# Second layer of a two-layer transformer: batch 0's residual inside batch 1's operand stage, batch 1's residual and the last normalisation as one stage

## The reference

```python
x = x + _layernorm(_L0_attn_ref(_layernorm(x), ...))
x = x + _layernorm(_L0_ffn_ref(_layernorm(x), ...))
x = x + _layernorm(_L1_attn_ref(_layernorm(x), ...))
x = x + _layernorm(_L1_ffn_ref(_layernorm(x), ...))
```

## Time and profile before

| | us |
|---|---|
| three runs, median (lowest, highest) | 3185.22 (3184.61, 3186.84) |
| profiled execution, its time | 3187.83 |
| profiled execution, its span | 3186.0 |

### The profile page before, as it was taken

How to read it: one execution, slowest core, us unless ns; L and a number is a source line. 1 busy time by engine, 2 the same in 40 slices (tenths; PEclk the granted TensorE clock), 3 DMA queues, 4 the chain that set the end, 5 groups by cost and what they waited for, 6 DMA issues and landing times. The chain is left out here.

```text
span 3186.0 us, 42804 instructions
## 1 busy us (share of the span) xinstructions
PE 2862.2 (90%) x14636; PEld 2289.0 (72%) x14636; DVE 1879.3 (59%) x3604; ACT 1231.7 (39%) x2366; POOL 990.2 (31%) x780
## 2 busy tenths in 40 slices
PE   7969999789999999458999999857999999499998
PEld 5846666568787878347788888656888888378886
DVE  5647787574453545445566666655666666644446
ACT  2226666562122212232444444322444444243334
POOL 1217777655453636305000000032000000122223
PEclk9979999889999999679999999979999999789999
DMA  4774444142121201671001000030000000300012
GB/s 165 239 212 142 121 129 125 56 142 83 42 64 41 64 24 34 212 291 74 18 23 35 23 23 35 29 140 28 24 23 35 23 23 30 126 21 20 10 37 80
DMA packets 138035, 244.06 MB, mean 77 GB/s; under 512 B 14417, under 2 KB 78929, under 8 KB 137393
## 3 DMA queue, kind: packets, MB, share of 16 engines
q1 hardware_dynamic: 137904, 242.40, 23.4%
HBM read 162.92 MB, written 79.17 MB: 76 GB/s over the span
## 5 line engine op out<-in xcount | busy, mean ns | idle before, releaser
L1094 POOL TENSOR_TENSOR l0a_probs_hl<-l0a_probs,l0a_probs_hl 128x896 fp32r<-128x896 f32 (+1 forms) x128 | 285.0, 2244 | 108.1 <-ACT l0a_probs L1022 108.1
L1352 ACT ACTIVATE l1a_probs<-l1a_scores,l1a_row 128x128 f32<-128x128 f32 (+7 forms) x256 | 189.6, 742 | 317.9 <-DVE l1a_row L1389 317.8
L1326 PE MATMUL l1a_obank<-l1a_pT_hl,l1k_v_hl 128*128 128x512 f32 (+3 forms) x1152 | 300.4, 370 | 7.2 <-DVE l1a_pT_hl L1399 7.1
L1442 POOL TENSOR_TENSOR l1a_q_stage<-l1k_qpe,l1a_ones 128x512 fp32r<-128x512 f32 x32 | 33.3, 1041 | 875.3 <-PE l1a_work L1334 818.4
L1399 DVE TENSOR_TENSOR l1a_pT_hl<-l1a_work,l1a_pT_hl 128x512 fp32r<-128x512 f32 (+3 forms) x384 | 213.2, 555 | 154.6 <-ACT l1a_pT_hl L1359 154.4
L1306 PE MATMUL l1a_scores<-l1k_kT_hl,l1a_qa_hl 128*128 128x512 f32 (+3 forms) x1152 | 291.6, 361 | 1.5 <-ACT l1a_probs L1352 1.5
L1359 ACT CAST l1a_pT_hl<-l1a_work 128x512 fp32r<-128x512 f32 (+3 forms) x384 | 183.7, 478 | 106.3 <-PE l1a_work L1317 105.2
L1334 PE MATMUL l1a_work<-l1a_wov,l1a_oT_hl 128*128 128x512 f32 x768 | 214.3, 401 | 5.0 <-DVE l1a_oT_hl L1418 3.0
L1389 DVE TENSOR_REDUCE l1a_row<-l1a_scores 128x1 f32<-128x128 f32 (+7 forms) x256 | 190.0, 751 | 44.5 <-PE l1a_scores L1309 44.4
L1413 DVE SCALAR_TENSOR_TENSOR l_acc<-l1a_work,l1a_row,l_acc 128x512 f32<-128x512 f32 x256 | 189.4, 750 | 34.4 <-PE l1a_work L1334 24.5
L1713 PE MATMUL f0f_ybank<-f0f_wT,f0f_h_hl 128*128 128x512 f32 x768 | 196.7, 406 | 12.7 <-POOL f0f_h_hl L1879 12.6
(11 more groups left out here) (255 smaller groups left out, 6200.0 us busy)
## 6 DMA issues: line engine op xcount, KB each, us to landing
v_dram<-l0f_v_rows SPq DMA_DIRECT2D x24, 768.0 KB, 4.0
qk_dram<-l0f_stage SPq DMA_DIRECT2D x128, 128.0 KB, 2.5
l1a_wov<-wov_dram SPq DMA_DIRECT2D x32, 512.0 KB, 3.4
l0a_v_stage<-v_dram SPq DMA_DIRECT2D x32, 384.0 KB, 4.3
l1a_wabs<-wabs_dram SPq DMA_DIRECT2D x32, 384.0 KB, 3.8
l0a_q_stack<-qk_dram SPq DMA_DIRECT2D x32, 256.0 KB, 3.6
l0a_k_stack<-qk_dram SPq DMA_DIRECT2D x32, 256.0 KB, 3.8
f0f_chunk<-in_L_ffn_w_gate_up SPq DMA_DIRECT2D x32, 256.0 KB, 2.7
```

What stands on the lines that cost most here:

```text
L1094: nc.gpsimd.tensor_tensor(probs_hl[:, r, 1, 0:wide], probs[:, r, 0:wide], f32(probs_hl[:, r, 0, 0:wide]), ALU.subtract).then_inc(low_done, 1)
L1326: last = pe.matmul(obank[:, c:SPAN], src["v_hl"][:, a, n, :], pT_hl[:, ring(n, s), b, c:SPAN], start=(n == 0 and i == 0), stop=(n == QT * ...
L1352: nc.scalar.activation(probs[s][:, first:first + wide, :].rearrange("p k c -> p (k c)"), scores[:, n % S_AHEAD, 0:wide * P], ACT.Exp, bias ...
```

## The change

- Batch 0's `residual` stage after its attention is dropped. `latent_operands` for batch 1 gets `rows`: per tile the statistics, a root on ScalarE, the inverse and a shift (minus mean times inverse) on VectorE, the row scaled by ScalarE in place in `acc`, the sum with `x2` on GpSimd in place, a store to `x3`. The two accumulators become one, `l1_acc`.
- Batch 1's `residual` stage and the `norm_transposed` before the feed-forward become `residual_norm_transposed`. Tiles of batch 0 come from `x3` (kind A), tiles of batch 1 from `acc` after their residual (kind B), in the order of `join_order`. Rows of both kinds are scaled by ScalarE.
- In `feed_forward` the last rows are scaled and summed in place in `acc`; the buffer `z` and its waits for stores go.

```diff
+def join_order():
+
+    order = [("A", k) for k in range(QT)]
+    for k in range(TB - QT):
+        order += [("A", QT + k), ("B", k)]
+    return order + [("B", k) for k in range(TB - QT, TB)]
...
+def residual_norm_transposed(nc, m, ident, done_rows, acc, src, dst, xT_hl, loads):
...
+            def inverse(which, n):
+                r = n % RING
+                dve.wait_ge(std_done[which], n + 1)
+                nc.vector.reciprocal(rstd[:, which, r:r + 1], std[:, which, r:r + 1]).then_inc(rstd_done[which], 1)
+                dve.wait_ge(rstd_done[which], n + 1)
+                nc.vector.scalar_tensor_tensor(out=shift[:, which, r:r + 1], in0=mv[:, which, r, 0:1], scalar=-1.0,
+                                               in1=rstd[:, which, r:r + 1], op0=ALU.mult, op1=ALU.mult
+                                               ).then_inc(shift_done[which], 1)
+
+            for i in range(N + LATER + 4):
+                j = i - LATER
+                if i < TB:
+                    statistics(0, i, acc[:, i, :])
+                if 0 <= j < N:
+                    kind, k = order[j]
+                    if kind == "A":
+                        dve.wait_ge(x0_loaded[k // QT], 16)
+                    else:
+                        dve.wait_ge(sum_done, k + 1)
+                    statistics(1, j, source(j))
+                if 0 <= i - 1 < TB:
+                    inverse(0, i - 1)
+                if 0 <= j - 1 < N:
+                    inverse(1, j - 1)
+                if i < TB:
+                    aggregate(0, i)
+                if 0 <= j < N:
+                    aggregate(1, j)
+                if 0 <= j - 4 < N:
+                    j = j - 4
+                    dve.wait_ge(high_done, j + 1)
+                    nc.vector.tensor_tensor(xT_hl[:, 1, :, tokens(j)],
+                                            bank[:, j % RING, :].rearrange("p (k t) -> p k t", k=KT),
+                                            f32(xT_hl[:, 0, :, tokens(j)]), ALU.subtract).then_inc(low_done, 1)
+            dve.wait_ge(low_done, N)
...
+            def scaled(which, n, to, rows):
+                r = n % RING
+                act.wait_ge(shift_done[which], n + 1)
+                return nc.scalar.activation(to, rows, ACT.Identity, bias=shift[:, which, r:r + 1],
+                                            scale=rstd[:, which, r:r + 1])
+
+            for i in range(N + LATER + 4):
+                if 0 <= i - 1 < TB:
+                    root(0, i - 1)
+                if 0 <= i - LATER - 1 < N:
+                    root(1, i - LATER - 1)
+                if 0 <= i - 2 < TB:
+                    k = i - 2
+                    scaled(0, k, acc[:, k, :], acc[:, k, :]).then_inc(z_done, 1)
+                if 0 <= i - LATER - 2 < N:
+                    j = i - LATER - 2
+                    wait(act, turned, j - 1)
+                    scaled(1, j, xn[:, j % 2, :], source(j)).then_inc(normed, 1)
+                if 0 <= i - LATER - 4 < N:
+                    j = i - LATER - 4
+                    act.wait_ge(turned, j + 1)
+                    nc.scalar.copy(xT_hl[:, 0, :, tokens(j)], bank[:, j % RING, :].rearrange("p (k t) -> p k t", k=KT)
+                                   ).then_inc(high_done, 1)
+
...
+                pool.wait_ge(z_done, k + 1)
+                pool.wait_ge(x1_loaded[k // QT], 16)
+                nc.gpsimd.tensor_tensor(acc[:, k, :], acc[:, k, :], x1[:, k, :], ALU.add).then_inc(sum_done, 1)
...
-                    wait(act, row_stored[b], 16 * half)
-                    nc.scalar.activation(z[:, b, :], acc[:, half * QT + b, :], ACT.Identity,
+                    nc.scalar.activation(acc[:, half * QT + b, :], acc[:, half * QT + b, :], ACT.Identity,
...
+def latent_operands(nc, m, ident, xT_hl, waT, wpT, norm_w, rope, out, stores=(), rows=None):
...
+            def load_row(t):
+                wait(sp, r_sum_done, t - 1)
+                sp.dma_start(x[:, t % 2, :], row_src[t * P:(t + 1) * P, :]).then_inc(r_loaded[t % 2], 16)
+
             for dst, tile in stores:
                 sp.dma_start(dst, tile).then_inc(stored, 16)
+            if rows is not None:
+                load_row(0)
+                load_row(1)
+                for t in range(TB):
+                    sp.wait_ge(r_sum_done, t + 1)
+                    sp.dma_start(row_dst[t * P:(t + 1) * P, :], acc[:, t, :]).then_inc(r_stored, 16)
+                    if t + 2 < TB:
+                        load_row(t + 2)
+                sp.wait_ge(r_stored, 16 * TB)
...
-            act.wait_ge(eps_set, 1)
-            for i in range(TB + 1):
+            act.wait_ge(eps_set, 1 if rows is None else 2)
+            for i in range(TB + 2):
+                if rows is not None and 1 <= i <= TB:
+                    t = i - 1
+                    act.wait_ge(r_mv_done, t + 1)
+                    nc.scalar.activation(r_std[:, t % 2:t % 2 + 1], r_mv[:, t % 3, 1:2], ACT.Sqrt, bias=eps_ln[:, 0:1]
+                                         ).then_inc(r_std_done, 1)
+                if rows is not None and i >= 2:
+                    t = i - 2
+                    act.wait_ge(r_shift_done, t + 1)
+                    nc.scalar.activation(acc[:, t, :], acc[:, t, :], ACT.Identity, bias=r_shift[:, t % 2:t % 2 + 1],
+                                         scale=r_inv[:, t % 2:t % 2 + 1]).then_inc(r_z_done, 1)
                 if i < TB:
                     t = i
                     act.wait_ge(d_full, t + 1)
...
+                if rows is not None and i < TB:
+                    t = i
+                    nc.vector.bn_stats(r_stats[:, t % 2, :], acc[:, t, :]).then_inc(r_stats_done, 1)
+                if rows is not None and 1 <= i <= TB:
+                    t = i - 1
+                    dve.wait_ge(r_std_done, t + 1)
+                    wait(dve, r_z_done, t - 1)
+                    nc.vector.reciprocal(r_inv[:, t % 2:t % 2 + 1], r_std[:, t % 2:t % 2 + 1]).then_inc(r_inv_done, 1)
+                    dve.wait_ge(r_inv_done, t + 1)
+                    nc.vector.scalar_tensor_tensor(out=r_shift[:, t % 2:t % 2 + 1], in0=r_mv[:, t % 3, 0:1], scalar=-1.0,
+                                                   in1=r_inv[:, t % 2:t % 2 + 1], op0=ALU.mult, op1=ALU.mult
+                                                   ).then_inc(r_shift_done, 1)
+                if rows is not None and i < TB:
+                    t = i
+                    dve.wait_ge(r_stats_done, t + 1)
+                    nc.vector.bn_aggr(r_mv[:, t % 3, :], r_stats[:, t % 2, :]).then_inc(r_mv_done, 1)
...
+                        pool.wait_ge(r_z_done, t + 1)
+                        pool.wait_ge(r_loaded[t % 2], 16 * (t // 2 + 1))
+                        nc.gpsimd.tensor_tensor(acc[:, t, :], acc[:, t, :], x[:, t % 2, :], ALU.add
+                                                ).then_inc(r_sum_done, 1)
...
                     kept.close()
                     with phase(f"l1a{b}") as m:
-                        attention_layer1(nc, m, ident, ident_bf, mask, ops, acc)
-                with phase(f"l1r{b}") as m:
-                    residual(nc, m, TB, x2[b * S:(b + 1) * S], x3[b * S:(b + 1) * S], lambda t: acc[:, t, :])
...
                 with phase("f1n") as m:
-                    norm_transposed(nc, m, ident, x3, NT, xT,
-                                    group_loads(raw1, 0, 0, *ffn1) + group_loads(raw1, 1, 1, *ffn1))
+                    residual_norm_transposed(nc, m, ident, x3[0:S], l1_acc, x2[S:2 * S], x3[S:2 * S], xT,
+                                             group_loads(raw1, 0, 0, *ffn1) + group_loads(raw1, 1, 1, *ffn1))
+                acc = x.sb("acc", [P, NT, D])
```

More of the change, by code:

```diff
@@ L1848, in run @@
                     dve.wait_ge(x_loaded[half % 2], 16 * (half // 2 + 1))
-                    nc.vector.tensor_tensor(z[:, b, :], z[:, b, :], x[:, half % 2, b, :], ALU.add).then_inc(sum_last, 1)
+                    row = acc[:, half * QT + b, :]
+                    nc.vector.tensor_tensor(row, row, x[:, half % 2, b, :], ALU.add).then_inc(sum_last, 1)
         each_group(dve, run, chunks is not None, rows is not None)
@@ L1898, in run @@
                     pool.wait_ge(x_loaded[half % 2], 16 * (half // 2 + 1))
-                    nc.gpsimd.tensor_tensor(z[:, b, :], z[:, b, :], x[:, half % 2, b, :], ALU.add).then_inc(sum_done, 1)
+                    row = acc[:, half * QT + b, :]
+                    nc.gpsimd.tensor_tensor(row, row, x[:, half % 2, b, :], ALU.add).then_inc(sum_done, 1)
         each_group(pool, run, chunks is not None, rows is not None)
@@ L2172, in latent_operands @@
     stored = m.sem("stored")
+    if rows is not None:
+        row_src, row_dst, acc = rows
+        x = m.sb("x", [P, 2, D])
+        r_stats, r_mv = m.sb("r_stats", [P, 2, 6]), m.sb("r_mv", [P, 3, 2])
+        r_std, r_inv, r_shift = (m.sb(n, [P, 2]) for n in ("r_std", "r_inv", "r_shift"))
+        eps_ln = m.sb("eps_ln", [P, 1])
+        r_loaded = [m.sem(f"r_loaded{i}") for i in range(2)]
```

(9 more changed lines are left out.)

83 lines of the change are left out of this document (74 added, 9 removed).

## The result

The changed kernel takes **3170.14 us** (median of five runs, 3168.19 to 3173.05), the kernel before 3185.22 (3184.29 to 3194.30) beside it. The ratio of the runs is 0.9948, 95% interval 0.9934 to 0.9963: faster by 0.5%. The prediction said 3173, range 3164 to 3181. The profiled execution has a span of 3168.4 us, 17.6 under that of before; its own time is the median.

The account below looks back on a forecast made before the run. TensorE, busy nine tenths of the span, was taken as the bound, with gains only where it stands still. -19.4 + 17.1 - 9.7 - 0.3 = -12.3 us gave a median of 3173 us, range 3164 to 3181.

Parts of the forecast that it names:

- Part 1: Between batch 0's attention and batch 1's norm stage: the residual stage goes, 19.4 us gained (bounds 18.7 and 20.1).
- Part 2: Batch 1's operand stage, which takes in batch 0's residual: 17.1 us paid (bounds 9.8 and 25).
- The loop: Operand stage: copy, VectorE's round, aggregate, square root, scaled row, next copy take 10.1 us instead of 7.93.
- Five steps: Operand stage: five of seven steps from copy to copy contain the rotary part, 5 x 2.15 = 10.8 us.
- the last two tiles: End of the operand stage: its last two rounds cost about 0.4 us more.
- rival C: Operand stage: TensorE falls to its lower clock, six rounds 35 us longer than forecast, 3208 us, slower; chance 0.04.
- The choice between a held and a free shift: Operand stage: shift taken as held until GpSimd's sum ends, 2.5 us after the crossing; free it ends after 1.0.
- A: Rival, operand stage: the shift isn't held by GpSimd's sum, residual costs 9.8 us, whole 3166 us; chance 0.15.
- Part 3: Joined stage of batch 1's residual and the norm: 47.0 us instead of 56.75, 9.7 gained (bounds 39 and 54).
- the eight rounds with both chains: Joined stage: 8 rounds at 3.1 us from the first layer's output stage, less early subtractions, 22.1 us.
- The tail: End of the joined stage, after the last aggregate: root, inverse, row, transposes, copy, subtraction and handovers, 3.7 us.
- Part 4: Feed-forward's rows in place: one wait for a store goes from the last group, 0.3 us gained.

Follow-up runs that it names:

- root_later: Against the changed kernel, ScalarE issues the residual's root and scaled row behind the casts of the operand stage's round: 3159.76 us, ratio to the kernel before 0.9914.
- shift_one_input: Against the changed kernel, the one-column shift is a tensor_scalar with one SBUF tensor in operand and joined stages: 3156.79 us, ratio to the kernel before 0.9904.

## Why the prediction was right, step by step

- **Part 1**, 19.4 us gained: 20.71 - 1.40 = 19.3. The handover with clearing took 1.4 where 1.3 was taken. The norm stage (b) kept its length, so the table load costs nothing.
- **Part 2**, 17.1 us paid: 18.2. The loop was 9.96 us for 10.1. Five steps gave 5 x 2.03 = 10.1 (10.8 less the 0.7 of VectorE's wait), the two before them 4.52 + 6.00 - 3.11 - 4.49 = 2.9 (3.3), the end 3.6 - 0.3 = 3.3 (3.4). The mis-sized term is the last two tiles, taken at 0.4: from the last copy to the end of the last rotary sum it is 25.7 us for 23.5, so 2.2. There TensorE was at its lower clock for a part of the products: the last two groups took 5.71 and 5.97 us for 4.36 each before (last section). The first copy came 0.3 us sooner after its product's start. It was rival C in a small form: not a loop at the lower clock, but two groups of products; in the rounds from 2123 to 2153 the granted clock was 1.00. What the prediction held against C, that waits of 2 to 2.6 us had left the clock at 1.00, didn't carry over: the group of 5.97 us stands behind the same wait of 2.60 us.
- **The choice between a held and a free shift**, on which A stood, was right: median 1.80 us. That root_later took back 12.9 us of part 2 by the order, and shift_one_input 7.2 by the shift, shows both links of the loop. A's own price of 9.8 us doesn't follow from its loop of 8.8: five steps of 1.3 us less take 6.5 off 17.1 and leave 10.6. With free shifts, in shift_one_input, stage (c) paid 87.44 - 76.39 = 11.05.
- **Part 3**, 47.0 us: 45.7. Handover 1.45 (1.3), 5.8 to the first rows of x (5.5). From there to the end of the last aggregate at 2777.7 it is 32.9 (35.7): 20.7 for the eight rounds with both chains (22.1) and 12.2 for the eight with one (13.6). Of the first eight, three went by before GpSimd's first add (2750.31) in 1.0, 1.9 and 1.9 us; the five after it took 2.5 to 4.3 us, 3.2 in the mean, with the seven held shifts (0.65 to 1.24 us each) among them. The 3.1 us a round, taken from another stage, was too much for the first three. Of the last eight, seven took 1.60 us each (1.7), and the last one ends with its aggregate, 1.0 us after it began. The tail is 4.7 (3.7), and the handover with the first wait 0.8 (0.8).
- **Part 4**, 0.3 us: the scaled rows now start 0.20 us after the last shift's start instead of 0.49. That is the 0.3 expected, and far too small for (f), which varies by 1.3 us in kernels with the same code.
- **Not in the sum:** attention 1 was 2.4 us shorter. Nothing in the prediction had it, and its cause stays open (last section).

By stages the changes of (a) to (f) are -19.3, -0.1, +18.2, -2.4, -11.0 and -1.1, together -15.7; the other 1.9 us of the 17.6 between the two spans come from ahead of attention 0's end, where the code is the same. Of the 12.3 us predicted, the part in (a), (c) and (e) was -12.0 and came out -12.1: 1.3 more gained in (e), 1.1 more paid in (c), 0.1 less in (a). The loop, the held shift and the full VectorE are as forecast, but that this sum fits to 0.1 us is luck: two misses of over 1 us cancel. That the whole came out 2.9 us lower than forecast is, to the size of the scatter, attention 1.

## What to carry to other kernels

Work that fits into an engine's idle time by amount can still close a loop by its place in the order. Before adding a chain to a pipelined round, follow it from engine to engine and ask whether its last link stands ahead of the round's first on an in-order engine: here moving two instructions of 1.1 us to the back of ScalarE's round was worth 12.9 us, at no cost. And a one-column VectorE operation with two SBUF tensors beside GpSimd should be written with one tensor and a per-partition scalar (0.21 us beside GpSimd, where it had taken 1.80).
